# Two attention layers with heads of 64: the score block moved from the head of a step to a place just before the mix

## What is computed

```python
x = x + _L2_xattn_ref(_layernorm(x, axis=-1), ctx_768, Wq, Wk, Wv, Wo, bo)
...
HEADS = 16
DIM_HEAD = 64
q = (x @ Wq).reshape(B, N, HEADS, DIM_HEAD).transpose(0, 2, 1, 3)
k = (context @ Wk).reshape(B, M, HEADS, DIM_HEAD).transpose(0, 2, 1, 3)
v = (context @ Wv).reshape(B, M, HEADS, DIM_HEAD).transpose(0, 2, 1, 3)
dots = jnp.einsum('bhnd,bhmd->bhnm', q, k) * SCALE
attn = jax.nn.softmax(dots, axis=-1)
out = jnp.einsum('bhnm,bhmd->bhnd', attn, v)
out = out.transpose(0, 2, 1, 3).reshape(B, N, HEADS * DIM_HEAD)
return out @ Wo + bo
```

## Time and profile before

| | |
|---|---|
| median of 3 runs | 1894.32 us (1894.15 to 1895.41) |
| the profiled execution | 1890.68 us |
| its span, first to last instruction | 1888.9 us |
| TensorE busy | 1775.6 us, 94% of the span |
| DVE, ACT, POOL busy | 1382.2, 1017.8, 496.5 us |
| mean granted TensorE clock | 0.982 of full speed |
| head loop of layer 2 | about 1038 to 1376 us |
| head loop of layer 3 | about 1462 to 1759 us |

### The profile page before, as it was taken

One profiled execution on the slowest core, in us unless ns is written; L12 is line 12 of the kernel. 1 busy time (PEld: TensorE's weight loads), 2 busy tenths in 40 slices (PEclk: granted clock), 3 DMA queues, 4 the chain that ended last, 5 costly groups with the idle time before them and its releaser, 6 DMA issues. The chain is left out here.

```text
span 1888.9 us, 31069 instructions
## 1 busy us (share of the span) xinstructions
PE 1775.6 (94%) x11692; PEld 1574.6 (83%) x11695; DVE 1382.2 (73%) x3118; ACT 1017.8 (54%) x2239; POOL 496.5 (26%) x522
## 2 busy tenths in 40 slices
PE   6869999999999999999977999999979999999698
PEld 6658898999999898999856888888867888888587
DVE  6478787878777787878685575757777777777786
ACT  4455555565555565555554464646623666666421
POOL 0613030302112030303001333333521433334242
PEclk9988999999999999999999999999989999999899
DMA  5100000000000000000021212020000000000111
GB/s 172 67 17 26 1 12 1 6 7 1 12 1 12 1 12 1 15 1 1 1 89 51 69 45 83 30 70 10 9 1 18 21 12 15 9 10 4 35 52 36
DMA packets 17749, 49.05 MB, mean 26 GB/s; under 512 B 2617, under 2 KB 7362, under 8 KB 15938
## 3 DMA queue, kind: packets, MB, share of 16 engines
q1 hardware_dynamic: 16738, 46.25, 7.4%
q10 hardware_dynamic: 864, 0.83, 0.1%
HBM read 46.15 MB, written 0.92 MB: 25 GB/s over the span
## 5 line engine op out<-in xcount | busy, mean ns | idle before, releaser
L1381 ACT ACTIVATE a_pH<-banks 125x512 fp32r<-125x512 f32 (+1 forms) x384 | 203.5, 544 | 268.0 <-PE banks L195 191.4
L1452 DVE TENSOR_TENSOR a_pL<-banks,a_pH 125x512 fp32r<-125x512 f32 (+1 forms) x384 | 235.4, 623 | 116.7 <-ACT a_pH L1381 114.8
L2000 POOL TENSOR_TENSOR a_prob<-a_prob,a_rinv 112x750 f32<-112x750 f32 x128 | 184.0, 1437 | 394.4 <-DVE a_rinv L2311 394.4
L1433 DVE TENSOR_SCALAR_CACHE_REDUCE a_prob<-banks 128x500 f32<-128x500 f32 x336 | 221.8, 676 | 5.0 <-PE banks L195 4.1
L1271 PE MATMUL banks<-ident,a_prob 128*125 128x128 f32 x1344 | 201.2, 274 | 6.6 <-ACT a_prob L1366 4.4
L1366 ACT ACTIVATE a_prob<-a_prob,a_nmax 128x1000 f32<-128x1000 f32 x168 | 187.9, 1121 | 32.8 <-DVE a_nmax L1436 32.8
L195 PE MATMUL banks<-a_pH,a_head_vH 125*128 125x256 f32 (+1 forms) x576 | 200.1, 347 | 5.2 <-DVE a_pL L1452 4.3
L1271 PEld LDWEIGHTS banks<-ident,a_prob 128*125 128x125 f32 x1344 | 186.4, 188 | 9.8 <-ACT a_prob L1366 4.9
L1225 POOL TENSOR_TENSOR a_head_oH<-a_o,ones 128x256 fp32r<-128x256 f32 (+1 forms) x24 | 16.4, 684 | 605.8 <-DVE a_o L1460 605.8
L195 PE MATMUL banks<-a_pH,a_head_vL 125*128 125x256 f32 (+1 forms) x576 | 173.1, 300 | 0.0
L195 PE MATMUL banks<-a_pL,a_head_vH 125*128 125x256 f32 (+1 forms) x576 | 172.5, 300 | 0.0
(11 more groups left out here) (414 smaller groups left out, 5065.8 us busy)
## 6 DMA issues: line engine op xcount, KB each, us to landing
a_w_out<-in_f_out SPq DMA_DIRECT2D x6, 1024.0 KB, 5.0
a_w_in<-in_f_in SPq DMA_DIRECT2D x12, 512.0 KB, 4.8
f_raw<-in_f_w SPq DMA_DIRECT2D x9, 513.0 KB, 3.6
pair_raw<-in_a_qk SPq DMA_DIRECT2D x16, 256.0 KB, 2.8
pair_raw<-in_a_w SPq DMA_DIRECT2D x8, 384.0 KB, 3.1
a_v<-in_ctx_rows SPq DMA_DIRECT2D x4, 576.0 KB, 7.7
a_kT<-in_f_w SPq DMA_DIRECT2D x2, 1024.0 KB, 5.8
pair_raw<-in_a_wv SPq DMA_DIRECT2D x8, 256.0 KB, 3.0
```

The costliest lines, as they stand in the source:

```text
L1381: act.activation(pH[:, c % RING, 0:wide], TB[c % 4][0:KB, 0:wide], ACT.Copy).then_inc(t_high, 1)
L1433: dve.tensor_scalar(prob[:, at, c * CHUNK:(c + 1) * CHUNK], SB[c % 3][:, 0:CHUNK], SCALE, None, ALU.mult, ALU.max, accum_out=chunk_max[:, ...
L1452: dve.tensor_tensor(pL[:, c % RING, 0:wide], TB[c % 4][0:KB, 0:wide], pH[:, c % RING, 0:wide].bitcast(F32), ALU.subtract).then_inc(t_done, 1)
L2000: pool.tensor_tensor(both, both, rinv[:, n % RING, :].unsqueeze(2).to_broadcast([SEQ, 2, KEYS]), ALU.mult).then_inc(p_normed, 1)
```

## The change

TensorE's order alone is changed. The score block goes to the end of the step, behind the pieces and ahead of the mix, and is that of n+4 in place of n+3; scores(0, 3) is issued before the loop. The second half of the queries of head h+1 is made in step b = 7 of head h, where it was made in b = 0 of its own head; for head 0 it stays in step 0. ACT, DVE and POOL keep their order of scores, exponentials and copies, with the queries' copies moved along.

```diff
-    QUERIES_AT = (3, 8)
+    QUERIES_AT = (3, 7)
...
     def queries_at(h, b):
-        return [(h, n) for n, at in enumerate(QUERIES_AT) if at == b + BATCH] \
-            + [(h + 1, n) for n, at in enumerate(QUERIES_AT) if at == b and h + 1 < HEADS]
+        return [(0, 1)] * (h == 0 and b == 0) + [(h + 1, n) for n, at in enumerate(QUERIES_AT) if at == b and h + 1 < HEADS]
...
             def step(h, b):
                 n = BATCH * h + b
-                if n + AHEAD < STEPS:
-                    scores(*divmod(n + AHEAD, BATCH))
                 if n + 1 < STEPS:
                     turn(n + 1)
                 for each in keys_at(h, b):
...
                 for each in experts_at(h, b):
                     combine(*each)
+                if n + AHEAD + 1 < STEPS:
+                    scores(*divmod(n + AHEAD + 1, BATCH))
                 mix(h, b)
...
             scores(0, 2)
             for u in (8, 9):
                 values(0, u)
+            scores(0, 3)
             for h in range(HEADS):
```

## The result

The changed kernel takes **1938.2 us** (median of 5 runs, 1934.2 to 1942.3) against 1894.2 us before (5 runs, 1890.4 to 1895.4): a ratio of 1.0239, interval 1.0226 to 1.0251. The forecast was 1932.9 us, range 1919 to 1943. The profiled execution has a span of 1936.4 us, 47.5 more than before.

What follows compares the result with a forecast made beforehand. TensorE, nearly always busy in the head loops, was taken as the bound. Stalls 42.6, removed waits -4.4 and -1.6, layer starts +2.0 and block boundaries 0 gave +38.6 us on 1894.3: 1932.9 us, range 1919 to 1943.

Steps and rivals of the forecast that it cites:

- The chain through ACT: Transpositions, ACT's copy of their result, then exponentials release the score block: never less than 2.92 us after the transpositions start.
- the list: Steps sorted by the work between transpositions and score block; 53 of 118 too short to cover the release, losing 42.6 us.
- T to S: From start of the six transpositions to start of the score block: at least 2.92 us in stalled steps.
- S to the next T: From score block start to next transpositions' start, with the mix between: 1.70 us, forecast at the layer's start.
- S to M: Switch from score block to mix: gap near 0.26 us, taken from score block to values, as no row showed it.
- rival 1: Switch from score block to mix costs only 0.11 us, saving 18 us over 118 steps: 1915 us, chance 8%.
- the boundaries: TensorE's switches between blocks in every step: net change 0, with bounds of -18 and +6 us.
- Rival 2: The score block never stalls, if exponentials run ahead of the turned copy: 1890 us (2%) or 1893 us (1%).
- Rival 3: DVE's maxima end later than 1.57 us after the transpositions start, adding the excess each such step: 1948 us, chance 6%.
- wait for oL at b = 2 and 3: Last heads' mixes waiting 0.91 and 0.76 us for the outputs' low part: would go, saving 4.4 us over both layers.
- qL waits, 1.6 us: Score block waits for the queries' low part in b = 1: would go as queries come earlier, saving 1.6 us.
- rival 4: Clock falls to 1.2 GHz in the last heads' emptier steps b = 2 and 3: +18 us as bound, 1951 us, chance 6%.

Runs made afterwards that it cites:

- by room: Changed kernel, but the score block precedes the mix only in steps with a values pair or experts (two pairs in b = 0), elsewhere heading the next step: 1896.3 us.
- the added copy in the old order: Kernel before, with one more ACT copy of 112x256 into a dead buffer each step, just ahead of the exponentials: 1904.3 us, ratio 1.0061.

## Why the prediction was right, and where not

**The step that carried it held.** The chain through ACT, read from one step of the last head, set the start of 53 score blocks, the steps were those of the list, and the idle time by kind came within 0.07 us of the forecast. With the measured idle times the list gives 11 x 1.37 + 8 x 0.95 + 0.86 + 9 x 0.60 + 20 x 0.25 + 4 x 2.15 = 42.5 us, against 42.6.

**Two terms were off and cancel, for it is the same 0.1 us moved.** T to S is 2.83, not 2.92, for T itself is shorter when it follows a mix: T to the next block takes 0.58 (1090.39 to 1090.97) where it took 0.67 behind a score block. In return S to the next T is 1.80, not 1.70: the mix is the one that now comes behind S and its first pair takes 0.21 (1093.93 to 1094.14). The block behind the score block pays this 0.1, T before and the mix now. S to M took 0.70, with 0.26 from the last matmul of S to the first of M, as assumed from the S to v row, so rival 1 (that pair is cheap) is out. The Trainium skill's rule that a change of tiling mode drains TensorE (TensorEngine Tiling (Array Packing), Key Properties) agrees with this: the cost stays with the switch, whichever block stands beside it. In unstalled steps the boundaries came out at nothing: k+v+v in layer 3 takes 6.02 to 6.05 from T to T before (6.08 where it stood in b = 7) and 6.03 or 6.04 after. Rival 2 (no stall) is out with the 2.83. Rival 3 (DVE falls behind) didn't come: in the k step behind k+o, T at 1351.22, the maxima ended 0.75 after T and the exponentials started at 1.48.

**What was to go, and the start.** In layer 3's and layer 2's last heads the mixes no longer wait for oL at b = 2 and 3, as said. Step 0 costs 1.1 more in layer 2 (T to T 6.06 against 4.97), where 1.0 was forecast. The "qL waits, 1.6 us" were mis-sized as a gain of the queries' move: alone it lengthens the two loops by 1.7 us, since b = 0 with o alone is itself held by ACT's chain. In the changed kernel that step stalls anyway and this is in the list.

**What is missing from the sum is the clock, rival 4.** From the first to the last T, layer 2's loop grew by 17.4 us (340.99 to 358.43) and layer 3's by 26.9 (299.60 to 326.54); the prediction's terms give 16.6 and 22.0. The kernel before has no half-clock stretch inside either loop. The changed one has the three shown at the start: 3.4 us near the end of layer 2's, and in layer 3's 3.4 us from step 0 on and 10.2 us in the last head. The start of the last one, in TensorE's timeline:

```profile
1786.45 0.27 PE L195 MATMUL banks<-a_pH,a_vL 125*128 125x224 f32 x1
1786.56 0.33 PE L195 MATMUL banks<-a_pL,a_vH 125*128 125x224 f32 x1
1786.69 0.42 PE L195 MATMUL banks<-a_pH,a_vH 125*128 125x224 f32 x1
...
1787.33 1.46 PE L2125 MATMUL banks<-ident,a_prob 112*125 112x112 f32 x6
1790.82 0.66 PE L2115 MATMUL banks<-kH,a_qH 64*112 64x376 f32 x2 [2.02 <-ACT a_prob L2209]
```

The pitch inside the mix doubles from 0.11 to 0.21. This is the mix of the first step without a piece: the score block ahead of it had waited 2.02 us, and the two steps before had been idle for 1.37 and 0.60 us. T, at the head of the chain, takes 0.65 longer, so that the next score block starts 3.48 after it. Against the same steps at full clock (layer 2's for step 0) this adds up to 1.1 + 0.5 in steps 0 and 1 and 0.3 + 2.1 + 0.9 in the last head, 4.9 us: the whole of 26.9 - 22.0. In layer 2 the step behind the last stall takes 3.93 us where it took 2.73, 1.2 more, against 17.4 - 16.6. So of the 44.3 us of both loops the forecast's mechanism gives about 38, near its 38.6, and the clock some 6. I had given the clock 6% as an alternative to the forecast; it came beside it, in a small dose. The step of the prediction that failed is there: it took the clock as all or nothing, by one row at 83% busy, where the new idle steps are at about 53%. That the idle steps bring the falls about is argued, not shown by a run of its own. For it: the four kernels whose longest wait of TensorE inside the loops is 1.2 us or less (the kernel before, the queries alone, by room, the added copy in the old order) have no half-clock stretch there, and the six with a wait of 2.0 us or more each have 6.8 us or more. Just when the clock falls stays open: after the same wait of 2.11 us in step 0 it fell in layer 3 and not in layer 2. The remaining 3.2 us of the profiled execution lie outside the two loops, in code that the change leaves alone; they differ as much between other runs here.

## What to carry to other kernels

When a block is moved ahead of another, ask which wait stands at its head and what work covered that wait until now; here 1.1 us of mix was the cover of a 2.9 us chain, and every step whose other work was shorter paid the difference. The length of such a chain is best read in the one place where nothing else covers it, an end of a loop, and then held against each kind of step. And a wait on one engine is shortened by its order only until the next engine's queue takes over: putting the exponentials first gave back 16 of 44 us, about half of what was expected, because later copies then made DVE's maxima, and with them the exponentials, late in steps like the one shown.

## What the hardware showed beyond that

The block behind the 64-row score block pays about 0.1 us in its first pair of matmuls, beside the 0.26 to 0.27 us before it; the transpositions take 0.58 us to the next block behind a mix and 0.67 behind the score block. And TensorE's clock fell to half within a loop: in layer 3 right after a wait of 2.02 us, in layer 2 only after two steps, one behind the other, with such a wait each (at 1383.86). It stayed full in the last heads of the kernel before, where TensorE was 83% busy and no wait was longer than 0.91 us.
